# A graph network's edge stage: a table built from its source in place, two result buffers, eight smaller gather parts, another order of work

## The chip, the cores and the metric

The kernel runs on one NeuronCore of a Trainium2 chip. The metric is the device time of one execution in microseconds (us), the median of several runs. TensorE is called PE here, VectorE DVE, ScalarE ACT, GpSimd POOL and SyncE SP.

## The reference, cut to what matters

The program is two graph layers on 50000 nodes with 16 features and 850000 edges sorted by target, each with a residual and a layer norm. The first layer works on groups of eight nodes and has a weight for each of five edge types; the second is two relational convolutions with eight edge types.

```
Wg  = W[edge_types - 1]                              # layer 0
msg = einsum('eoi,eib->eob', Wg, xr[src])
y   = segment_sum(msg, dst) + segment_sum(Bv[edge_types - 1], dst)
x   = layernorm(x + y)
for r in range(8):                                   # layer 1, done twice
    msg = msg + where(edge_type == r, x[src] @ W[r], 0)
agg = segment_sum(msg * norm, dst);  h = agg + x @ root + bias
x   = layernorm(x + log_softmax(h))
```

## The kernel before, in words

Instead of multiplying each edge's source row by its type's weight, the kernel first writes a table in DRAM: for each node (or group of eight) one row per edge type, already multiplied. A layer then gathers one table row per edge and sums by target. The program is a chain of stages with a barrier between them: stage_edges, stage_sum0, stage_x1, stage_layer (l1), stage_middle, stage_layer (l2), stage_output.

stage_edges does four things side by side, each engine by a list of instructions written out by hand and held together by semaphores.

1. The table of layer 0. `x_sb` holds the source, 49 tiles of 128 groups (WINS0 = 49). For each tile ACT copies the tile into a staging buffer `xt` (L266), PE transposes it (L308), ACT copies the transposed tile back (L274), PE multiplies it with `mix` and adds the bias row by a matmul with one row (L317, L318; 512 + 128 columns), ACT copies the result from PSUM to `out` (L278, L279), and SP stores `out` (L214). `xt`, `x_turned`, `turn_ps` and `out` have two buffers each, `mul_ps` has one.
2. The steps. The 7040 steps by which the layers walk over the edges are found from the last target of each tile of 128 edges: DVE counts (L368, L371), PE sums the counts over the partitions with one matmul (L300, `bend_ps`), DVE compares and counts again (L387 to L402, `steps_ready`), then fills the small step tables (to L425, `tables_ready`).
3. The local targets of each step. POOL gathers the target rows of the steps (L108 by way of `fetch`, 64 indirect DMAs in PARTS = 4 parts of 16) into one buffer `got`, DVE subtracts the window's first node (L441), PE transposes in 16 batches of four (L340), ACT casts them into `env.local` (L291). Part b may be gathered when part b-1 has been transposed (`got_turned`).
4. The lists of table rows, one for layer 0 and one for layer 1. DVE computes `flat` (L429 to L435, L450), PE transposes it in 13 batches (L329), ACT casts them into `typ6` or `typ8` (L285), SP stores them (L227, L229).

PE's order is: L300, the whole table, the whole list of layer 0, the 16 batches of local targets, the list of layer 1. ACT's order is the same. On SP the loads of x, of the targets and of the edge lists stand ahead of the 49 stores of the table, and the small step tables and the lists' stores stand behind them.

The class Table builds the tables of layers 1 and 2 (in stage_x1 and stage_middle) in the same manner, with staging copies (L649), a transpose (L627), a copy back (L655) and matmuls of 512 + 512 + 128 columns (L638), but with two result buffers, and with DVE reading a part of each result (L675, L677).

## Time and profile before

| what | value |
|---|---|
| median of 3 runs | 19951.57 us (19948.39 to 19953.89) |
| the profiled execution | 19956.64 us |
| its span | 19954.9 us |
| PE, DVE, ACT, POOL busy | 44%, 20%, 1%, 69% of the span |
| stage_edges | from 0 to 531.57 us of the span |

The span is the time from the first to the last instruction of the profiled execution; the rest of its time lies around it. All start times below are us from the span's start. PEld is PE's weight load, which overlaps its matmuls; a matmul in f32 is issued as two passes, and a transpose as one. Engines whose name ends in q are the engine's queue, which issues waits and DMAs.

### The profile page before, as it was taken

What the parts mean: (1) busy time and instruction counts of PE and PEld (TensorE: products, weight loads), DVE (VectorE), ACT (ScalarE), POOL (GpSimd) and SP (SyncE); (2) the same over time, 40 slices, a digit from 0 to 9 for tenths busy, and PEclk for the clock granted to TensorE, in tenths of its full rate; (3) what the DMA queues carried; (4) which work ended last, traced back from release to release, by engine and by line L of the source; (5) the groups of instructions that cost most, each with busy time, mean ns of one, the idle gap of its engine ahead of it and who ended that gap; (6) DMA issues with size and microseconds to landing.
All of it is one profiled execution on the core that took longest, in us unless ns stands there. A gap on an engine that the chain in (4) does not pass through costs nothing. (4 is left out here: it accounts for less than half of the span.)

```text
span 19954.9 us, 176031 instructions
## 1 busy us (share of the span) xinstructions
PE 8832.7 (44%) x35275; PEld 7745.8 (39%) x35276; DVE 3970.6 (20%) x4654; ACT 265.0 (1%) x590; POOL 13732.8 (69%) x14217
## 2 busy tenths in 40 slices
PE   6565054444444444444445444444444444444444
PEld 2343054344334433444344333443344434443444
DVE  2223921111111111111112211111111111111113
ACT  1000000000000000000000000000000000000000
POOL 1672877777777777777770577777777777777760
PEclk9556555555555555555555655555555555555555
DMA  2122100000000000000000300000000000000000
GB/s 80 53 53 97 9 8 7 7 7 7 7 7 7 7 7 7 7 7 7 7 7 1 64 7 7 7 7 7 7 7 7 7 7 7 7 7 7 7 6 7
DMA packets 659119, 295.78 MB, mean 15 GB/s; under 512 B 351447, under 2 KB 628204, under 8 KB 657794
## 3 DMA queue, kind: packets, MB, share of 16 engines
q0 software_dynamic: 455680, 168.10, 7.7%
q1 hardware_dynamic: 202690, 124.50, 2.5%
q14 instruction: 317, 2.60, 0.0%
q8 instruction: 30, 0.49, 0.0%
q10 hardware_dynamic: 402, 0.09, 0.0%
HBM read 207.97 MB, written 87.17 MB: 15 GB/s over the span
## 5 line engine op out<-in xcount | busy, mean ns | idle before, releaser
L108 POOL DMA_INDIRECT l_rows<-table,l_idx x13312 | 12862.2, 966 | 4952.9 <-issue 4054.7
L988 PE MATMUL l_ps<-l_rows,l_hot 128*128 x28160 | 6326.9, 375 | 0.0
L988 PEld LDWEIGHTS l_ps<-l_rows,l_hot 128*128 128x128 f32 x28160 | 6137.4, 330 | 395.0 <-issue 395.0
L985 PE MATMUL l_ps<-l_zero 1*128 1x128 f32 x3520 | 1339.9, 482 | 9697.2 <-issue 9627.7
L985 PEld LDWEIGHTS l_ps<-l_zero 1*128 1x128 f32 x3520 | 872.8, 306 | 9835.7 <-issue 9758.4
L1019 DVE TENSOR_TENSOR all_big<-all_big,l_ps 128x128 f32 x1760 | 506.8, 288 | 10839.5 <-PE l_ps L988 10839.5
L1025 DVE TENSOR_TENSOR l_hot<-l_ps,all_local 128x1024 f32<-128x1024 f32 x1760 | 2123.7, 1217 | 5.8 <-issue 5.6
L108 POOL DMA_INDIRECT s_rows<-table,s_idx x832 | 785.6, 944 | 320.7 <-issue 251.3
L1038 DVE TENSOR_TENSOR l_rows<-l_rows,l_ps 128x1024 f32<-128x1024 f32 x208 | 254.0, 1221 | 3542.8 <-DMA l_rows<-table,l_idx 3542.2
L514 PE MATMUL s_ps<-s_zero 1*128 1x512 f32 x448 | 343.8, 906 | 440.1 <-issue 378.2
L517 PEld LDWEIGHTS s_ps<-s_rows,s_hot 128*128 128x128 f32 x1792 | 373.4, 317 | 140.8 <-issue 140.8
L517 PE MATMUL s_ps<-s_rows,s_hot 128*128 x1792 | 403.6, 416 | 0.0
L108 POOL DMA_INDIRECT ed_got<-dst_d,ed_step_i x64 | 83.8, 1310 | 406.7 <-PE ed_turn_ps L340 282.1
L514 PEld LDWEIGHTS s_ps<-s_zero 1*128 1x128 f32 x448 | 107.1, 264 | 558.6 <-issue 543.1
L539 DVE TENSOR_TENSOR early_acc<-early_acc,s_ps 128x1024 f32 x112 | 136.8, 1221 | 875.7 <-PE s_ps L517 875.7
L815 PE MATMUL l_ps<-all_ident,all_big 128*128 128x128 f32 x52 | 14.0, 433 | 349.3 <-DVEq L904 347.6
L815 PEld LDWEIGHTS l_ps<-all_ident,all_big 128*128 128x128 f32 x52 | 9.4, 218 | 353.6 <-DVEq L904 347.7
L318 PE MATMUL ed_mul_ps<-ed_bias_row,ed_one_row 1*128 1x512 f32 x196 | 140.3, 817 | 0.0
L317 PE MATMUL ed_mul_ps<-ed_mix,ed_x_turned 128*128 128x512 f32 x196 | 135.9, 797 | 1.2 <-ACT ed_x_turned L274 1.0
L545 DVE TENSOR_TENSOR s_hot<-s_iota_ps,all_local 128x1024 f32<-128x1024 f32 x112 | 134.0, 1217 | 3.9 <-issue 3.9
L649 ACT COPY midt_xt<-all_big 128x128 f32<-128x128 f32 x49 | 15.1, 310 | 8530.4 <-DVEq L1080 8530.4
L1109 ACT ACT_TABLE_LOAD x7 | 9.0, 1283 | 8752.9 <-PEq L90 8752.8
(172 smaller groups left out, 1815.0 us busy)
## 6 DMA issues: line engine op xcount, KB each, us to landing
l_rows<-table,l_idx POOLq DMA_INDIRECT x13312, 2.3
table<-midt_out SPq DMA_DIRECT2D x49, 512.0 KB
table<-x1t_out SPq DMA_DIRECT2D x48, 512.0 KB, 2.7
table<-ed_out SPq DMA_DIRECT2D x48, 320.0 KB, 2.1
s_rows<-table,s_idx POOLq DMA_INDIRECT x832, 2.6
idx_d<-ed_typ SPq DMA_DIRECT2D x2, 3328.0 KB, 9.4
l_idx<-idx_d SPq DMA_DIRECT2D x208, 32.0 KB, 1.8
ed_typ<-in_edge_type_dram SPq DMA_DIRECT2D x2, 2912.0 KB
```

The costliest lines, as they stand in the source:

```text
L108: pool.indirect_dma_start(out=out[:, j, :], out_offset=None, in_=table, in_offset=bass.IndirectOffsetOnAxis(ap=idx[:, j:j + 1], axis=0)).t ...
L317: nc.tensor.matmul(mul_ps[:, k, 0:z - a], x_turned[:, t % 2, :], mix[:, a:z], start=True, stop=False)
L318: last = nc.tensor.matmul(mul_ps[:, k, 0:z - a], one_row[:, :], bias_row[:, a:z], start=False, stop=True)
L514: nc.tensor.matmul(ps[g % 2][:, c * 512:(c + 1) * 512], zero[:, 0:P], zero[:, :], start=True, stop=False, skip_group_check=True)
L517: last = nc.tensor.matmul(ps[g % 2][:, bass.ds((v % GROUP) * ROW0, ROW0)], hot[:, g % 2, j, :], rows[:, bass.ds(v // GROUP, 1), :].rearran ...
L539: nc.vector.tensor_tensor(at, at, ps[g % 2][:, :].rearrange("n (w f) -> n w f", f=ROW0), ALU.add).then_inc(added, 1)
L545: nc.vector.tensor_tensor(hot[:, g % 2, :, :], iota_ps[:, 0:P].unsqueeze(1).to_broadcast([P, GROUP, P]), local.unsqueeze(2).to_broadcast([ ...
L985: nc.tensor.matmul(sums[g % 2], zero[:, :], zero[:, :], start=True, stop=False, skip_group_check=True)
L988: last = nc.tensor.matmul(sums[g % 2][:, bass.ds((v % GROUP) * FEAT, FEAT)], hot[:, g % 2, j, :], rows[:, bass.ds(v // GROUP, 1), :].rearr ...
L1019: nc.vector.tensor_tensor(at, at, sums[g % 2].rearrange("n (w f) -> n w f", f=FEAT), ALU.add).then_inc(added, 1)
L1025: nc.vector.tensor_tensor(hot[:, g % 2, :, :], lane_ps.unsqueeze(1).to_broadcast([P, GROUP, P]), local.unsqueeze(2).to_broadcast([P, GROUP ...
L1038: nc.vector.tensor_tensor(at, at, scale_ps.unsqueeze(2).to_broadcast([P, SPAN, FEAT]), ALU.mult).then_inc(scaled, 1)
```

## The change

In stage_edges:
- PE transposes the table's source straight from `x_sb`; the staging copies, their buffer and their semaphore go. The class Table loses them too, in both tables that it builds.
- `mul_ps` gets a second buffer; PE may multiply tile t when tile t-2 has been read. `bend_ps` no longer has a bank of its own and uses that of a list buffer. ACT turns back tile t before it reads the result of tile t-1.
- DVE makes `mix` and `bias_row` before it counts, no longer after; PE starts the table when these and x are there.
- L300 moves from the front of PE's list to behind tile 15 (EARLY = 16), and the two-tile loop is begun anew behind it.
- `got` gets a second buffer; PARTS goes from 4 to 8, so a part is 8 gathers and has half the size. Part b waits for part b-2 to be transposed.
- Behind the table PE and ACT do parts 0 and 1 of the local targets, six batches of list 0, part 2, the other seven batches, parts 3 to 7, list 1.

```diff
-PARTS = 4
+PARTS = 8
+EARLY = 16
...
-        got = s.sb("got", [P, SPAN // PARTS, P], I32)
+        got = s.sb("got", [P, 2, SPAN // PARTS, P], I32)
...
-        mul_ps = s.ps("mul_ps", [P, 2, 512])
-        bend_ps = s.ps("bend_ps", [P, 512])
+        mul_ps = [s.ps(f"mul_ps{b}", [P, 2, 512]) for b in range(2)]
         wide_ps = [s.ps(f"wide_ps{b}", [P, 4, P]) for b in range(2)]
+        bend_ps = wide_ps[0][:, :, :].rearrange("p a b -> p (a b)")
...
             for b in range(PARTS):
-                if b:
-                    pool.wait_ge(got_turned, b * part // 4)
-                fetch(pool, got[0:SPANS], rows, step_i[0:SPANS, b * part:(b + 1) * part], part, got_in[b])
+                if b > 1:
+                    pool.wait_ge(got_turned, (b - 1) * part // 4)
+                fetch(pool, got[0:SPANS, b % 2], rows, step_i[0:SPANS, b * part:(b + 1) * part], part, got_in[b])
...
         @block.scalar
...
+            def table_rows(a, z):
+                for t in range(a, z):
+                    act.wait_ge(turned, t + 1)
+                    if t > 1:
+                        act.wait_ge(multiplied, t - 1)
+                    nc.scalar.copy(x_turned[:, t % 2, :], turn_ps[t % 2][:, 0:P]).then_inc(back, 1)
+                    if t > a:
+                        read(t - 1)
+                read(z - 1)
...
+            table_rows(0, EARLY)
+            table_rows(EARLY, WINS0)
             act.wait_ge(idx0_ready, 1)
...
+            local_slots(0)
+            local_slots(1)
+            turned_lists(typ6, 0, 0, 6)
+            local_slots(2)
+            turned_lists(typ6, 0, 6, batches)
+            for b in range(3, PARTS):
+                local_slots(b)
             act.wait_ge(idx1_ready, 1)
-            turned_lists(typ8, batches)
+            turned_lists(typ8, batches, 0, batches)
...
         @block.tensor
...
+            pe.wait_ge(x_in, 32)
 
             def turn(t):
-                pe.wait_ge(staged, t + 1)
                 if t > 1:
                     pe.wait_ge(back, t - 1)
-                nc.tensor.transpose(turn_ps[t % 2][:, 0:P], xt[:, t % 2, :], env.ident[:, :]).then_inc(turned, 1)
...
+                nc.tensor.transpose(turn_ps[t % 2][:, 0:P], x_sb[:, t, :], env.ident[:, :]).then_inc(turned, 1)
+
+            def table_rows(a, z):
+                turn(a)
+                for t in range(a, z):
+                    if t + 1 < z:
+                        turn(t + 1)
+                    pe.wait_ge(back, t + 1)
+                    if t > 1:
+                        pe.wait_ge(read_out, t - 1)
+                    for k, (c, d) in enumerate(((0, 512), (512, width))):
+                        nc.tensor.matmul(mul_ps[t % 2][:, k, 0:d - c], x_turned[:, t % 2, :], mix[:, c:d],
+                                         start=True, stop=False)
+                        last = nc.tensor.matmul(mul_ps[t % 2][:, k, 0:d - c], one_row[:, :], bias_row[:, c:d],
+                                                start=False, stop=True)
+                    last.then_inc(multiplied, 1)
...
+            table_rows(0, EARLY)
+            pe.wait_ge(below_ready, 1)
+            nc.tensor.matmul(bend_ps[:, 0:WINS], ones[:, :], below[:, :], start=True, stop=True
+                             ).then_inc(bend_ready, 1)
+            table_rows(EARLY, WINS0)
             pe.wait_ge(back, WINS0)
...
+            local_slots(0)
+            local_slots(1)
+            pe.wait_ge(steps_ready, 1)
+            turn_lists(idx0_ready, 0, 0, 6)
+            local_slots(2)
+            turn_lists(idx0_ready, 0, 6, batches)
+            for b in range(3, PARTS):
+                local_slots(b)
+            turn_lists(idx1_ready, batches, 0, batches)
```

## Rows read from the trace of the kernel before

**Rows 1.** Busy time by stretch: us, PE, PEld, DVE, ACT, POOL, PEclk, DMA share, GB/s.

```profile
78.70:389.00 310.30, 262.49 (x417) 100.41 (x418) 55.35 (x26) 52.00 (x185) 35.38 (x16) 1.00 0.14 52
389.00:531.57 142.57, 37.94 (x166) 26.11 (x164) 13.97 (x5) 61.15 (x42) 48.43 (x48) 0.56 0.20 70
```

**Rows 2.** Timeline, one tile of layer 0's table: start us, us, what [idle before].

```profile
66.91 0.59 ACT L278 COPY ed_out<-ed_mul_ps 128x512 f32<-128x512 f32 x1 [5.62 <-PE ed_mul_ps L318]
...
67.55 0.31 ACT L266 COPY ed_xt<-ed_x_sb 128x128 f32<-128x128 f32 x1
...
67.91 0.48 PE L308 MATMUL ed_turn_ps<-all_ident,ed_xt 128*128 128x128 f32 x1 [1.04 <-ACT ed_xt L266]
```

**Rows 3.** Timeline: first staging copy, first store, third tile's read.

```profile
22.11 0.50 ACT L266 COPY ed_xt<-ed_x_sb 128x128 f32<-128x128 f32 x2 [15.38 <-DMA ed_x_sb<-in_x_dram]
...
60.95 0.36 SPq L214 DMA_DIRECT2D table<-ed_out  x1
...
78.71 0.59 ACT L278 COPY ed_out<-ed_mul_ps 128x512 f32<-128x512 f32 x1 [10.68 <-DMA table<-ed_out]
```

**Rows 4.** Busy time by stretch, columns as in rows 1.

```profile
76.00:80.00 4.00, 0.28 (x2) 0.29 (x2) 4.00 (x1) 1.12 (x4) 0.00 (x0) 1.00 0.09 32
```

**Rows 5.** Timeline, last tile to last gather of stage_edges.

```profile
388.24 0.59 ACT L278 COPY ed_out<-ed_mul_ps 128x512 f32<-128x512 f32 x1 [5.61 <-PE ed_mul_ps L318]
...
389.34 14.60 ACT L285 CAST ed_typ<-ed_wide_ps 128x512 int32<-128x512 f32 x13 [0.35 <-PE ed_wide_ps L329]
...
409.22 1.01 POOL L108 DMA_INDIRECT ed_got<-dst_d,ed_step_i  x1 [261.24 <-PE ed_turn_ps L340]
...
440.39 1.01 POOL L108 DMA_INDIRECT ed_got<-dst_d,ed_step_i  x1 [10.45 <-PE ed_turn_ps L340]
...
491.22 1.01 POOL L108 DMA_INDIRECT ed_got<-dst_d,ed_step_i  x1 [0.30 <-issue]
```

**Rows 6.** Timeline, last subtraction and first VectorE instruction of the next stage.

```profile
493.77 2.29 DVE L441 TENSOR_TENSOR ed_got<-ed_got,ed_step_w 110x2048 f32<-110x2048 int32 x1 [28.83 <-DMA ed_got<-dst_d,ed_step_i]
...
531.57 0.48 DVE L526 MEMSET s_zero<- 1x512 f32 x1 [27.77 <-PEq L90]
```

**Rows 7.** Timeline: the counting matmul, the first gather, the first subtraction.

```profile
52.12 1.64 PE L300 MATMUL ed_bend_ps<-ed_below,ed_ones 128*128 128x391 f32 x2 [52.12 <-DVEq L373]
...
108.02 1.18 POOL L108 DMA_INDIRECT ed_got<-dst_d,ed_step_i  x1 [106.26 <-DVEq L402]
...
149.85 2.29 DVE L441 TENSOR_TENSOR ed_got<-ed_got,ed_step_w 110x2048 f32<-110x2048 int32 x1 [17.20 <-DMA ed_got<-dst_d,ed_step_i]
```

**Rows 8.** Timeline of PE: list transposes, and matmuls of layer 1's table.

```profile
388.14 1.97 PE L329 MATMUL ed_wide_ps<-all_ident,ed_flat 128*128 128x128 f32 x8
...
395.48 0.66 PE L329 MATMUL ed_wide_ps<-all_ident,ed_flat 128*128 128x128 f32 x4 [0.25 <-ACT ed_typ L285]
...
503.91 1.97 PE L329 MATMUL ed_wide_ps<-all_ident,ed_flat 128*128 128x128 f32 x8 [1.48 <-DVEq L452]
...
1796.44 4.21 PE L638 MATMUL x1t_mul_ps<-x1t_mix,x1t_x_turned 128*128 128x512 f32 x6
...
1803.09 2.10 PE L638 MATMUL x1t_mul_ps<-x1t_mix,x1t_x_turned 128*128 128x512 f32 x6
```

**Rows 9.** Busy time by stretch, columns as in rows 1.

```profile
504.00:508.00 4.00, 3.41 (x14) 2.66 (x15) 0.00 (x0) 3.86 (x4) 0.00 (x0) 0.50 0.00 0
```

**Rows 10.** Timeline of VectorE and GpSimd, one gather beside a tensor_tensor.

```profile
125.56 7.09 DVE L435 TENSOR_TENSOR ed_flat<-ed_flat,ed_typ 128x6656 f32<-128x6656 f32 x1
...
125.95 7.58 POOL L108 DMA_INDIRECT ed_got<-dst_d,ed_step_i  x1 [0.31 <-issue]
```

**Rows 11.** Waits, the middle table: who waited for whom, us, times, longest.

```profile
ACT midt_out L667 <- DMA table<-midt_out: 61.0, 46, 3.1
...
PEld midt_turn_ps L627 <- ACT midt_xt L649: 8.3, 18, 1.9
```

**Rows 12.** The page's DMA issues: transfers, KB each, median us to landing.

```profile
table<-ed_out SPq DMA_DIRECT2D x48, 320.0 KB, 2.1
```

More of the change, by code:

```diff
@@ L260, in _, with read @@
             act.dma_start(env.ident[:, :], env.eye).then_inc(small_in, 16)
-            act.wait_ge(x_in, 32)
-            def stage(t):
-                if t > 1:
-                    act.wait_ge(turned, t - 1)
-                nc.scalar.copy(xt[:, t % 2, :], x_sb[:, t, :]).then_inc(staged, 1)
-            stage(0)
-            for t in range(WINS0):
-                if t + 1 < WINS0:
-                    stage(t + 1)
-                act.wait_ge(turned, t + 1)
-                if t > 1:
-                    act.wait_ge(multiplied, t - 1)
-                nc.scalar.copy(x_turned[:, t % 2, :], turn_ps[t % 2][:, 0:P]).then_inc(back, 1)
+            def table_rows(a, z):
[7 more added lines that the diff above has]
+                read(z - 1)
+            def read(t):
                 act.wait_ge(multiplied, t + 1)
@@ L363, in _ @@
             st.wait()
-            cmp = flat[:, :].bitcast(BF16)
-            for a, z in ((0, 256), (256, WINS)):
-                n = z - a
-                view = cmp[:, 0:n * PER].rearrange("p (w k) -> p w k", k=PER)
-                st(nc.vector.tensor_tensor(view, last_w[:, :].unsqueeze(1).to_broadcast([P, n, PER]),
-                                           win_id[:, a:z].unsqueeze(2).to_broadcast([P, n, PER]), ALU.is_le))
-                st.wait()
-                st(nc.vector.tensor_reduce(below[:, a:z], view, AX.X, ALU.add))
-                st.wait()
-            dve.sem_inc(below_ready, 1)
             dve.wait_ge(small_in, 16 * (CH + 2))
@@ L384, in _ @@
             dve.sem_inc(mix_ready, 1)
+            cmp = flat[:, :].bitcast(BF16)
+            for a, z in ((0, 256), (256, WINS)):
+                n = z - a
+                view = cmp[:, 0:n * PER].rearrange("p (w k) -> p w k", k=PER)
+                st(nc.vector.tensor_tensor(view, last_w[:, :].unsqueeze(1).to_broadcast([P, n, PER]),
+                                           win_id[:, a:z].unsqueeze(2).to_broadcast([P, n, PER]), ALU.is_le))
+                st.wait()
+                st(nc.vector.tensor_reduce(below[:, a:z], view, AX.X, ALU.add))
+                st.wait()
+            dve.sem_inc(below_ready, 1)
             dve.wait_ge(bend_ready, 1)
@@ L643, in act @@
         nc = self.nc
-        act.wait_ge(self.values_ready, 1)
-        def stage(t):
-            if t > 1:
-                act.wait_ge(self.turned, t - 1)
-            nc.scalar.copy(self.xt[:, t % 2, :], self.values[:, t, :]).then_inc(self.staged, 1)
         def turn_back(t):
@@ L655, in turn_back @@
             nc.scalar.copy(self.x_turned[:, t % 2, :], self.turn_ps[t % 2][:, 0:P]).then_inc(self.back, 1)
-        stage(0)
-        stage(1)
         turn_back(0)
@@ L661, in act @@
                 turn_back(t + 1)
-            if t + 2 < WINS0:
-                stage(t + 2)
             act.wait_ge(self.multiplied, t + 1)
```

77 lines of the change are left out of this document (29 added, 48 removed).

## The prediction, made before the changed kernel had run

> **What bounds the kernel.** I read the page first: the two layer stages run at the pace of GpSimd's gathers, and this change touches neither, so its worth has to be read in stage_edges, which ends where the next stage's first VectorE instruction starts, 531.57 us into the span [rows 6], and in the two tables built by class Table. Then the busy times by stretch, to see who is dense where. From 78.7 to 389 us PE is busy 262.49 of 310.30 us: the table of layer 0 [rows 1]. From 389 to 531.57 it is busy 37.94 of 142.57, and the stretch is a relay of GpSimd, VectorE, PE and ScalarE [rows 1].
>
> In the first stretch the timeline of one tile shows the loop. ScalarE reads the single result buffer after 5.62 us of waiting for PE, then stages the source, turns back, and PE idles 1.04 us until the staging copy [rows 2]. The last 46 reads span 388.24 - 78.71 us, so a tile takes 6.73 us, and PE works for 6.73 - 1.04 = 5.69 of it [rows 2, 3, 5]. The first two tiles are special: the third tile's read waits 10.68 us for the store of the first, until 78.71 [rows 3], and the DMA share has fallen to 0.09 just then [rows 4]: the edge lists' loads stand ahead of the table's stores.
>
> In the second stretch the turning of list 0 (14.60 us on ScalarE) comes first, and the second part of the step gathers starts only at 409.22, after four turned batches [rows 5]. A gather takes 1.01 + 0.30 = 1.31 us. Between two parts of 16 GpSimd waits 10.45 us, since one buffer holds a part until it is turned [rows 5]. The last gather starts at 491.22; 2.55 us later VectorE subtracts, the list of layer 1 is made, turned and stored, and the stage ends at 531.57 [rows 5, 6].
>
> **The change, part by part.**
>
> *Earlier start.* The mix is built ahead of the counting and PE waits for x alone, so tile 0 can start at about 22.1, where the first staging copy starts now [rows 3]. Two tiles fit into the two `out` buffers, two more into the result buffers, then ScalarE waits for the first store. That one is queued on the same SP ring behind the same loads, so it lands about when it does now; I take 78.71 (bounds 76 to 80, the stretch in which the DMA engines run empty) [rows 3, 4]. The start 32 us earlier is worth two tiles, not 32 us.
>
> *Two result buffers, no staging.* The loop of a tile then holds only PE's own 5.69 us: the idle 1.04 goes with the staging copy and the read [rows 2]. Turning back tile t and reading tile t-1 (about 1.1 us of ScalarE a tile) lie under the 5.6 us of the other buffer's matmuls. After 78.71: read and turn-back 1.1, then tile 4 and 44 more at 5.69: 78.71 + 1.1 + 45 x 5.69 = 335.9. The moved matmul L300 (1.64 us [rows 7]) and the restart of the two-tile pipeline behind it, some 1.0, add 2.6: PE ends the table at 338.4. It ends now with the read at 388.24, so 49.8 us are won. Bounds: 5.64 (a tile packed tighter) to 5.8 us, 333 to 345.
>
> *Later steps.* L300 goes from 52.12 to behind tile 15, at 79.8 + 12 x 5.69 = 148. VectorE queues behind it everything from the steps on, and GpSimd waits for that: gathers now start at 108.02 and the first subtraction is at 149.85 [rows 7]. All this moves 96 us later, the first 16 gathers to 204 to 246. It costs nothing while the table covers it: PE wants them at 338. Cover left: about 90 us; without it each microsecond costs one. The mix's wait for the small loads now stands ahead of the counting on VectorE; a delay there has the same cover.
>
> *Order behind the table.* Parts 0 and 1 (16 gathers) are ready, so PE turns two batches at once, and GpSimd may start part 2: 2.0 us (eight passes [rows 8]) plus 0.3 after 338.4, at 340.7. Now that start is 21.0 us behind the last read (409.22 - 388.24), because list 0 and four batches come first. List 0 is put between the parts: 13 batches at 14.60/13 = 1.12 us plus 16 local batches at 2.0 are 47 us of ScalarE in some 70 us of gathers, hidden. The tightest place is part 5's start, behind the last seven list batches (7.9 us) and part 3; I find 3 to 4 us of slack there, and take 0 (bounds 0 and 5). SP's store of list 0 now falls beside gathers; they issue on another queue and have 5 us before they are wanted: 0.
>
> *Two gather buffers.* Six parts of eight, 48 gathers without the two gaps of 10.45: 47 x 1.31 = 61.6 us to the last start. Against it stands what GpSimd loses to VectorE: the gather at 125.95 took 7.58 us in place of 1.01, until 0.9 us after a tensor_tensor that read two SBUF operands [rows 10]. The subtraction L441 is such an operation. Now GpSimd stands idle while it runs; with two buffers five of them (parts 2 to 6, half of 2.29 = 1.15 us each) run while GpSimd gathers: 5 x 1.15 = 5.75 us. I take it in full, since the row shows a whole stall; bounds 0 and 7. In the Trainium skill, SBUF — State Buffer, Who interferes with whom, a tensor_tensor with two SBUF inputs is said to contend with a GpSimd instruction that reads SBUF, while a probe is reported in which tensor_tensor did not stall a DMA issued there. By the probe the term would be 0 and the sum 5.75 lower; the trace here disagrees with the probe, 7.58 us against 1.01.
>
> *Tail.* From L441 to the stage's end 531.57 - 493.77 = 37.8, now with half the subtraction: 36.65 [rows 6]. Sum: 340.7 + 61.6 + 5.75 + 2.55 + 36.65 = 447.3 against 531.57: 84.3 us won.
>
> *The other tables.* In the middle table ScalarE waits for a store 46 times of 49, 61.0 us in all; the loads of PE that wait for a staging copy, 18 with 8.3 us, follow those waits [rows 11]. Removing the copy does not make a store land earlier: the first tile's staging, about 0.5 us in each table, is sure. I take 1 us for both (bounds: 4 lost by a clock that falls in another place, 8 won).
>
> Total 85.3. The profiled execution took 19956.6 us (span 19954.9), 5 above the median of the runs, 19951.6; the difference is set against the median: **19866 us**.
>
> **The rivals.**
>
> *The clock rises* (0.06). PE would now be without a gap for 250 us. The trace prints 1.00 throughout the table, but eight passes of a transpose take 1.97 at 388.14 and the same 1.97 at 503.91, where the clock's row says 0.50, and from 395.48 four take 0.66 [rows 8, 9]. So I read the table as run at the lower level, 1.2 GHz, and the 1.00 as a state that was not recorded before the first change. At 2.4 GHz a tile would take half (in the next table six passes go from 4.21 to 2.10 us [rows 8]): the last 44 tiles 125 us less, the stage's end at about 322, 19741 us. For it: the idle 1.04 us disappears. Against it: PE was 85% busy for 310 us [rows 1] and the clock didn't rise; it rose only some 7 us after the work had changed to transposes that use all rows, while two of the four matmuls of a tile, here and after, use a single row (L318). The Trainium skill, TensorE: Matmul & The Clock Gate, Part 1, says that sustained activity releases the throttle and asks for no gaps; by it the table would run at the higher level and give this 19741.
>
> *The result buffer isn't the limit* (0.05): the tile stays at 6.73, since ScalarE's order binds. The table ends at 391, only the second stretch is won, 32 us: 19919. Against it: the class Table has two result buffers and its passes follow without a gap there, 2.10 us a tile [rows 8].
>
> *The parts stall on each other* (0.04): each part waits until the one before is turned behind list batches, 7 us for six parts: 42 lost, 19908.
>
> *Slower, stores that pile up* (0.03): the stores of the table leave from 29 us on and land as late as the first does now, 17.7 us after the copy (60.95 to 78.7 [rows 3]), for the whole table. With two `out` buffers a tile would take 8.9 us, the table would end at 488, and the stage at 597: 65 slower, 20017. It decides from about 7.5 us a tile, landings over 15 us. Against it: a store of 320 KB lands in 2.1 us by the median, and the DMA share behind 78.7 is 0.14 [rows 1, 12].
>
> **How the numbers follow.** My forecast has 0.80; 0.02 is left for what I don't see. Its own range: 6 less without the lock, 5 less and 7 more from the tile's pace and the store, 5 from the hand-over of parts, -7 to +5 from the other tables: 19848 to 19884. The range given, 19836 to 19897, adds some room for a cost that no row shows; the rivals at 19741, 19908, 19919 and 20017 (0.18) lie outside. A change below 0.2% (40 us) counts as none. Faster: 0.80 + 0.06, part of the two rivals near the bound and half of the unseen, 0.89; same 0.07; slower 0.04.
>
> **What the changed profile would show.** First matmul of the table near 22 us, a PE gap from about 46 to 80, then a read every 5.7 us; L300 near 148; GpSimd's first gather near 204; the table's end near 338; the seventeenth gather at 341, gathers up to 7 stretched by about 1.2 us each by L441; the next stage's first VectorE instruction near 447; the other two tables within 4 us of before. A tile of 2.9 us, a first store that lands far from 79, or waits of GpSimd between parts would each make a term wrong.

## The result and the profile after

| what | before | after |
|---|---|---|
| median (5 runs each, side by side) | 19952.75 us (19948.39 to 19954.55) | 19850.43 us (19844.47 to 19854.65) |
| ratio, 95% interval | | 0.9949 [0.9934, 0.9963] |
| the profiled execution, its span | 19956.64, 19954.9 us | 19848.08, 19846.3 us |
| stage_edges ends | 531.57 us | 434.45 us |

The change wins 102.3 us by the medians, 0.5%. The forecast was 19866, 15.6 above the measurement, which lies in the range (19836 to 19897) and in the forecast's own (19848 to 19884). By the two profiles stage_edges is 97.1 us shorter, and the rest of the span 11.5. Line numbers below are those of the changed kernel: L313 is the transpose, L324 and L326 the matmuls, L267 turns back, L276 and L277 read the result, L352 counts, L109 gathers, L462 subtracts.

Busy time by stretch after the change, in the columns of [rows 1]:

```profile
22.00:46.00 24.00, 23.22 (x38) 8.70 (x38) 23.93 (x3) 2.32 (x8) 0.00 (x0) 1.00 0.97 259
46.00:77.50 31.50, 0.00 (x0) 0.00 (x0) 7.91 (x2) 0.01 (x1) 0.00 (x0) 1.00 0.89 216
77.50:331.00 253.50, 252.39 (x408) 95.72 (x409) 80.38 (x29) 42.77 (x138) 35.39 (x16) 1.00 0.17 63
331.00:434.45 103.45, 40.51 (x167) 29.80 (x165) 14.52 (x7) 62.35 (x44) 49.73 (x48) 1.00 0.30 96
```

PE works from 22 to 46 us, is idle for 31.5 us, and is then busy 252.39 of 253.50 us: the table runs without a gap. The DMA share is 0.97 and 0.89 in the first two stretches, 0.70 from 70 to 74 us and 0.11 from 76 to 77.5: the engines run empty just before the third read.

The timeline of ScalarE at the third tile's read, which answers to [rows 3]; of PE there and one tile later; of ScalarE at the last read, which answers to [rows 5]:

```profile
77.49 0.58 ACT L276 COPY ed_out<-ed_mul_ps 128x512 f32<-128x512 f32 x1 [42.70 <-DMA table<-ed_out]
```
```profile
78.47 2.07 PE L324 MATMUL ed_mul_ps<-ed_mix,ed_x_turned 128*128 128x512 f32 x2 [33.11 <-ACT ed_x_turned L267]
80.47 2.07 PE L326 MATMUL ed_mul_ps<-ed_bias_row,ed_one_row 1*128 1x512 f32 x2
82.47 0.80 PE L324 MATMUL ed_mul_ps<-ed_mix,ed_x_turned 128*128 128x128 f32 x2
83.20 0.79 PE L326 MATMUL ed_mul_ps<-ed_bias_row,ed_one_row 1*128 1x128 f32 x2
83.92 0.47 PE L313 MATMUL ed_turn_ps<-all_ident,ed_x_sb 128*128 128x128 f32 x1
84.19 1.92 PE L324 MATMUL ed_mul_ps<-ed_mix,ed_x_turned 128*128 128x512 f32 x2
...
89.48 0.47 PE L313 MATMUL ed_turn_ps<-all_ident,ed_x_sb 128*128 128x128 f32 x1
```
```profile
330.59 0.58 ACT L276 COPY ed_out<-ed_mul_ps 128x512 f32<-128x512 f32 x1 [4.70 <-PE ed_mul_ps L326]
```

From transpose to transpose a tile takes 89.48 - 83.92 = 5.56 us, against 6.73 before. The start comes 32 us earlier and then waits 42.70 us for the first store.

The second half: the first gather behind the table, the only two that take longer than 1.15 us from there on, and the last; VectorE's subtractions beside them; the stage's end, which answers to [rows 6]:

```profile
332.51 1.01 POOL L109 DMA_INDIRECT ed_got<-dst_d,ed_step_i  x1 [91.67 <-PE ed_turn_ps L347]
...
346.98 1.36 POOL L109 DMA_INDIRECT ed_got<-dst_d,ed_step_i  x1 [0.30 <-issue]
...
355.22 1.01 POOL L109 DMA_INDIRECT ed_got<-dst_d,ed_step_i  x1 [0.30 <-issue]
...
372.30 1.94 POOL L109 DMA_INDIRECT ed_got<-dst_d,ed_step_i  x1 [0.30 <-issue]
...
395.57 1.01 POOL L109 DMA_INDIRECT ed_got<-dst_d,ed_step_i  x1 [0.30 <-issue]
```
```profile
346.24 1.23 DVE L462 TENSOR_TENSOR ed_got<-ed_got,ed_step_w 110x1024 f32<-110x1024 int32 x1 [102.58 <-DMA ed_got<-dst_d,ed_step_i]
355.20 1.28 DVE L462 TENSOR_TENSOR ed_got<-ed_got,ed_step_w 110x1024 f32<-110x1024 int32 x1 [7.74 <-DMA ed_got<-dst_d,ed_step_i]
372.13 1.23 DVE L462 TENSOR_TENSOR ed_got<-ed_got,ed_step_w 110x1024 f32<-110x1024 int32 x1 [15.65 <-DMA ed_got<-dst_d,ed_step_i]
...
398.20 1.22 DVE L462 TENSOR_TENSOR ed_got<-ed_got,ed_step_w 110x1024 f32<-110x1024 int32 x1 [9.26 <-DMA ed_got<-dst_d,ed_step_i]
...
434.45 0.48 DVE L547 MEMSET s_zero<- 1x512 f32 x1 [27.71 <-PEq L91]
```

48 gathers follow without a wait between parts (0.30 us of issue each), 63.1 us from the first start to the last.

### The profile page after: what moved, and what is told of

It is laid out like the page before. It is cut to its first block and busy times, and to the rows that moved or that the text cites. A ratio compares the mean times of both kernels' runs of the same rounds, so it can differ in the third digit from the quotient of the medians.

```text
span 19846.3 us, 175756 instructions
## 1 busy us (share of the span) xinstructions
PE 8826.6 (44%) x35275; PEld 7745.4 (39%) x35276; DVE 3972.9 (20%) x4658; ACT 236.6 (1%) x443; POOL 13724.6 (69%) x14217
## 5 line engine op out<-in xcount | busy, mean ns | idle before, releaser
L109 POOL DMA_INDIRECT l_rows<-table,l_idx x13312 | 12853.3, 966 | 4950.9 <-issue 4056.6
L109 POOL DMA_INDIRECT s_rows<-table,s_idx x832 | 785.1, 944 | 319.3 <-issue 251.1
L109 POOL DMA_INDIRECT ed_got<-dst_d,ed_step_i x64 | 85.1, 1330 | 309.7 <-DVEq L423 199.1
L324 PE MATMUL ed_mul_ps<-ed_mix,ed_x_turned 128*128 128x512 f32 x196 | 133.6, 785 | 33.4 <-ACT ed_x_turned L267 33.1
L326 PE MATMUL ed_mul_ps<-ed_bias_row,ed_one_row 1*128 1x512 f32 x196 | 140.3, 817 | 0.0
L869 DVE TENSOR_SCALAR_CACHE_REDUCE all_big<-all_big 128x6656 bf16<-128x6656 bf16 x16 | 113.4, 7086 | 0.6
```

What stands on the lines that cost most here:

```text
L109: pool.indirect_dma_start(out=out[:, j, :], out_offset=None, in_=table, in_offset=bass.IndirectOffsetOnAxis(ap=idx[:, j:j + 1], axis=0)).t ...
L324: nc.tensor.matmul(mul_ps[t % 2][:, k, 0:d - c], x_turned[:, t % 2, :], mix[:, c:d], start=True, stop=False)
L326: last = nc.tensor.matmul(mul_ps[t % 2][:, k, 0:d - c], one_row[:, :], bias_row[:, c:d], start=False, stop=True)
```

## The experiments

All times of stages are from one profiled execution each, us of the span; "stage end" is the first instruction of the next stage, as 434.45 above. Edits are to the changed kernel where nothing else is said; line numbers in their rows can stand a few off those above, and some diffs show only a part of the edit, marked by "...". One thing scatters from profile to profile whatever the edit, the landing of the table's first store, and so the third read: in the nine profiles with the early start and the loads in their old place (the changed kernel's and those of eight runs below) it lies between 72.51 and 79.47 us, and the table's end moves with it. Differences of up to 7 us between last reads or stage ends are therefore read from the third read on, or behind the last read.

### The table's half alone

```diff
-PARTS = 8
+PARTS = 4
...
-        got = s.sb("got", [P, 2, SPAN // PARTS, P], I32)
+        got = s.sb("got", [P, 1, SPAN // PARTS, P], I32)
...
-            local_slots(0)
-            local_slots(1)
-            turn_lists(idx0_ready, 0, 0, 6)
-            local_slots(2)
-            turn_lists(idx0_ready, 0, 6, batches)
-            for b in range(3, PARTS):
+            turn_lists(idx0_ready, 0, 0, batches)
+            for b in range(PARTS):
                 local_slots(b)
```

> The changed kernel with the gather side put back: four parts of 16 gathers, one gather buffer, list 0 ahead of all local targets. Only the table half of the change is left (source in place, two result buffers, early mix, the counting matmul behind tile 15). Theory, the two halves add up: the table ends at about 331 us as in the changed kernel, and the relay behind it takes what it took before, 531.57 - 388.24 = 143.3 us, so the stage ends at 474, 57 us earlier than before, and the kernel is at about 19888 us. Rival, the halves need each other (the later steps cost something when the parts are large): the stage ends later than 480.

19892.17 us, ratio 0.997 [0.9959, 0.9981]. Last read 325.61, stage end 468.04: 63.5 us of the 97.1. Some 5 us of that are the first store's, since the third read is at 72.51 in this profile and at 77.49 in the changed kernel's. Behind the last read the stage takes 142.4 us here, 143.3 before and 103.9 in the changed kernel. So the table's half carries some 58 us and the gathers' half 39; by the medians the second is 41.7.

### One result buffer

```diff
-        mul_ps = [s.ps(f"mul_ps{b}", [P, 2, 512]) for b in range(2)]
+        mul_ps = [s.ps("mul_ps0", [P, 2, 512])] * 2
...
-                    if t > 1:
-                        pe.wait_ge(read_out, t - 1)
+                    if t:
+                        pe.wait_ge(read_out, t)
```

> The changed kernel with one result buffer in stage_edges; PE may multiply a tile when the tile before has been read. Theory, the second result buffer gives the tile's pace: PE waits for the two reading copies (0.65 us and the hand-over), a tile takes about 6.2 to 6.3 us in place of 5.56, the table ends some 32 us later, the stage at about 466, the kernel at about 19882. Rival, the pace came from leaving out the staging copies: a tile stays below 5.8 us and the stage ends at 435 to 445.

19899.17 us, 0.9972 [0.9961, 0.9983]; last read 374.50, stage end 478.06. PE's timeline of one tile:

```profile
90.36 0.47 PE L313 MATMUL ed_turn_ps<-all_ident,ed_x_sb 128*128 128x128 f32 x1
91.36 2.04 PE L324 MATMUL ed_mul_ps<-ed_mix,ed_x_turned 128*128 128x512 f32 x2 [0.53 <-ACT ed_out L277]
...
96.78 0.47 PE L313 MATMUL ed_turn_ps<-all_ident,ed_x_sb 128*128 128x128 f32 x1
```

With the staging copy gone but one buffer, PE waits for the read of the result, and a tile takes 6.42 us. That is more than the 6.2 to 6.3 expected, and the stage ends 12 us later than expected. Of the 1.17 us by which the tile became shorter, staging and ScalarE's new order are 0.31 and the second buffer, put in behind them, 0.86; the second buffer with the staging kept was not run.

### The staged tables of the class Table

The class Table is that of the kernel before; stage_edges is as changed.

> The changed kernel with the class Table as it was before (staging copies in the tables of layers 1 and 2), stage_edges unchanged. In the two profiles the stage of layer 1's table went from 194.1 to 191.2 us and the middle table's span from 126.9 to 123.0 us. Theory, that is the staging: with it back the two are 194 and 127 within 1 us. Rival, it is where the clock and the stores happened to fall: they come out at 191 and 123, or scattered by several us. In both cases stage_edges ends at 434 to 435 and the kernel is within 10 us of the changed one.

19852.71 us, 0.995 [0.9933, 0.9967], 2.3 us over the changed kernel, whose own runs spread over 10. The two stages that build these tables (the second read up to the issue of its last store) took 191.24 and 122.95 us in the profile of the changed kernel, 193.03 and 127.69 here, 194.19 and 126.80 before. Over the eleven profiles with the unstaged class the first lies between 189.56 and 193.68 (mean 191.7) and the second between 122.73 and 127.04 (124.8); over the three with the staged one, this, the kernel before and its variant below, the means are 193.5 and 127.0. That is some 2 us a table, less than what single profiles scatter (4 us in each of the two).

### The late start

The mix is built behind the counting again, and the counting matmul stands at the front of PE's list.

```diff
+            pe.wait_ge(below_ready, 1)
+            nc.tensor.matmul(bend_ps[:, 0:WINS], ones[:, :], below[:, :], start=True, stop=True
+                             ).then_inc(bend_ready, 1)
...
-            table_rows(0, EARLY)
-            pe.wait_ge(below_ready, 1)
-            nc.tensor.matmul(bend_ps[:, 0:WINS], ones[:, :], below[:, :], start=True, stop=True
-                             ).then_inc(bend_ready, 1)
-            table_rows(EARLY, WINS0)
+            table_rows(0, WINS0)
```

> The changed kernel with the old front: the counting, then the counting matmul, then the mix, then the table in one piece, so PE starts the table at about 54 us, not 22. Theory, the start is worth next to nothing, since ScalarE waits for the first store until 77.5 in the changed kernel and 78.7 before: the third tile is read at about 78.7, the restart behind tile 15 (2.1 us) falls away, and the stage ends at 433 to 436. Rival, the 32 us of earlier start count: the stage ends at 445 to 465.

19851.98 us, 0.9948 [0.9932, 0.9965]; last read 327.02, stage end 431.78, 2.7 us earlier than the changed kernel's. PE's first matmul of the table is at 54.31 in place of 22.76, and the steps' first gather at 107.7 again. The third read is at 75.96, and the fourth follows at 76.76 as in the changed kernel (78.29 behind 77.49): four tiles are ready when the first store lands, in either case. From the third read to the last it takes 251.1 us in place of 253.1, since the two-tile loop is not begun anew. The early start and the move of the counting matmul are worth nothing here.

### The steps later still

`EARLY = 40`, one execution.

> The changed kernel with EARLY = 40: the counting matmul stands behind tile 39, at about 279 us in place of 145, so all steps come 134 us later, the first gather at about 335. Theory, the later steps are covered for some 87 us (in the changed kernel the second part's subtraction ends at 243.7 and PE wants it at 331) and cost one for one beyond: 134 - 87 = 47 us if every gather waits, somewhat less (about 41) since later parts follow without a gap. The stage ends at 475 to 482. Rival, there is no such cover (the changed kernel already lost some of it): the stage ends near 434 + 134 = 568. Rival, the steps are not on the path at all: 435 to 440.

The counting matmul runs at 276.17, the first gather at 332.07, stage end 474.14: 39.7 us later. The steps moved 131.2 us and cost 39.7. From the first gather to the last (435.31) GpSimd never waits in this run, so each further microsecond would cost one, and the cover in the changed kernel was 131.2 - 39.7 = 91.5 us, against "about 90" in the prediction. Outside stage_edges this execution shows both layer stages some 17 us longer, which the edit does not touch.

### A second operation that reads two SBUF operands

```diff
+                if 2 <= b < PARTS - 1:
+                    st(nc.vector.tensor_tensor(x_sb[:, 0:32, :], x_sb[:, 0:32, :], x_sb[:, 0:32, :], ALU.max))
```

> The changed kernel, and behind the subtraction of parts 2 to 6 VectorE does one more operation that the result doesn't need: a tensor_tensor of 4096 elements with two SBUF operands (about 4.3 us each, on the table's source, which is no longer wanted). Theory A, a gather that begins while such an operation runs is held until its end, whatever the length: each of the five adds 3 to 4.3 us to the gathers, 15 to 21 us in all, gathers of 4 to 5 us are seen, the last gather starts at 410 to 416 in place of 395.6, the stage ends at 450 to 456. Theory B, a tensor_tensor does not hold gathers and the two longer gathers of the changed kernel (1.36 and 1.94 us) have another cause: the last gather starts at 395 to 397 and the stage ends at 434 to 436.

One execution: last gather 411.96, 16.4 us later, stage end 450.20. VectorE and GpSimd side by side:

```profile
346.28 1.28 DVE L462 TENSOR_TENSOR ed_got<-ed_got,ed_step_w 110x1024 f32<-110x1024 int32 x1 [100.94 <-DMA ed_got<-dst_d,ed_step_i]
347.70 4.42 DVE L469 TENSOR_TENSOR ed_x_sb<-ed_x_sb 128x4096 f32<-128x4096 f32 x1
```
```profile
347.62 1.01 POOL L109 DMA_INDIRECT ed_got<-dst_d,ed_step_i  x1 [0.31 <-issue]
348.93 4.08 POOL L109 DMA_INDIRECT ed_got<-dst_d,ed_step_i  x1 [0.30 <-issue]
353.32 1.01 POOL L109 DMA_INDIRECT ed_got<-dst_d,ed_step_i  x1 [0.30 <-issue]
```

The gather that begins 0.08 us ahead of the long operation takes 1.01 us; the next begins inside it and ends at 353.01, 0.89 us behind the operation's end at 352.12. So a gather that begins inside is held until the operation is over, and what it loses is what is left of it. From restart to last gather it takes 78.8 us in place of 63.1.

### The same with a reduction

```diff
+                if 2 <= b < PARTS - 1:
+                    st(nc.vector.tensor_reduce(last_w[:, 0:32], x_sb[:, 0:32, :], AX.X, ALU.max))
```

> As the run with the additional tensor_tensor, but the additional operation is a tensor_reduce over the same 4096 elements, of the same length, with one SBUF operand. Theory A, only the second SBUF operand (or a fast mode) holds the gathers: the last gather starts at 395 to 397 and the stage ends at 434 to 436. Rival, any long VectorE operation holds them: 410 to 416 and 450 to 456.

One execution: last gather 395.35, stage end 434.19, as without the operation. It too takes 4.42 us (345.88 to 350.30), and the gathers beside it take 1.01. From restart to last gather it takes 64.5 us, 1.4 more than in the changed kernel, and all of that stands beside the subtractions: four gathers of 1.30 to 2.03 us. It is the kind of operation that holds a gather, not its length. What of the kind does it these two runs don't separate: the reduction has one SBUF operand in place of two, and writes 32 elements in place of 4096. A second SBUF operand is not needed, as the changed kernel's own trace shows at an earlier place:

```profile
203.68 4.03 POOL L109 DMA_INDIRECT ed_got<-dst_d,ed_step_i  x1 [0.30 <-issue]
```
```profile
203.96 3.63 DVE L450 TENSOR_SCALAR ed_flat<-ed_typ 128x6656 f32<-128x6656 int32 x1 [0.22 <-DVE ed_step_w L444]
```

This tensor_scalar reads one SBUF operand. The gather begins 0.28 us ahead of it, ends at 207.71, 0.12 us behind it, and takes 4.03 us. The kernel's total, 19889.02, is not read here: both layer stages are some 16 us longer in this execution as well.

### The edge lists' loads on another queue

```diff
-            sp.wait_ge(padded, 5)
-            load_list(sp, src, env.src, src_in)
-            load_list(sp, typ6, env.type6, type6_in)
-            load_list(sp, typ8, env.type8, type8_in)
...
+            act.wait_ge(x_in, 32)
+            act.wait_ge(padded, 5)
+            load_list(act, src, env.src, src_in)
+            load_list(act, typ6, env.type6, type6_in)
+            load_list(act, typ8, env.type8, type8_in)
```

> The changed kernel with the loads of the three edge lists issued by ScalarE (behind its wait for x) and no longer by SP, so that the table's stores no longer stand behind them in SP's queue. Theory, the first store waited for its place in the queue: now it lands well before 77.5, at 40 to 55 us, PE's idle stretch of 33 us shrinks to 0 to 15, the table ends 20 to 30 us earlier (about 303 to 311), and the stage ends at 405 to 415. Rival, it waited for the DMA engines' bandwidth, which are busy until about 75 whoever issues: the first store still lands near 77, and the stage ends at 432 to 440.

19848.25 us, 0.9945 [0.9928, 0.9962]. The stores of the table no longer stand behind these loads on SyncE's queue, and still the third read comes only at 71.22, 6.3 us earlier than in the changed kernel's profile and 1.3 below the lowest of the nine; the fourth waits again:

```profile
71.22 0.59 ACT L277 COPY ed_out<-ed_mul_ps 128x512 f32<-128x512 f32 x1 [32.86 <-DMA table<-ed_out]
...
75.68 0.59 ACT L277 COPY ed_out<-ed_mul_ps 128x512 f32<-128x512 f32 x1 [3.53 <-DMA table<-ed_out]
```

The DMA share is 1.03 from 22 to 46 us and 0.96 from 46 to 71.2. The first store waits for the engines' bandwidth far more than for its place in a queue. The stage ends at 423.51, 10.9 us earlier in the profiles; by the medians the kernel is 2.2 us faster, which is inside the spread. Of the 12.1 us by which the last read (318.5) is earlier, 6.3 are the store's; the rest is a short rise of the clock, which the edit did not ask for. PE's timeline behind tile 15, where the counting matmul (L353) and a new start of the loop put passes that use all rows side by side, and the busy times with the granted clock:

```profile
138.70 1.67 PE L353 MATMUL ed_wide_ps<-ed_below,ed_ones 128*128 128x391 f32 x2
...
144.60 0.34 PE L314 MATMUL ed_turn_ps<-all_ident,ed_x_sb 128*128 128x128 f32 x1
...
147.61 0.33 PE L314 MATMUL ed_turn_ps<-all_ident,ed_x_sb 128*128 128x128 f32 x1
...
151.70 0.47 PE L314 MATMUL ed_turn_ps<-all_ident,ed_x_sb 128*128 128x128 f32 x1
```
```profile
146.00:148.00 2.00, 2.00 (x8) 0.97 (x8) 2.00 (x1) 0.28 (x1) 0.00 (x0) 1.00 0.42 164
200.00:320.00 120.00, 120.00 (x201) 46.46 (x200) 21.58 (x6) 20.49 (x65) 30.61 (x14) 0.50 0.18 64
```

The tile from 144.60 to 147.61 takes 3.01 us; the clock falls at about 149 while PE goes on without a gap, and from then on it stands recorded at 0.50 with tiles of 5.56 us, the same as in the changed kernel, whose column prints 1.00. The run with the reduction shows the same rise at the same place (one tile of 4.24 us); the other profiles of this front don't.

### The bias matmul over all rows

`one_row` becomes 128 rows with a one in the first and zeros below, `bias_row` the same with the bias: the same sum, made by a matmul that uses all rows of the array.

```diff
-        bias_row = s.sb("bias_row", [1, width])
-        one_row = s.sb("one_row", [1, P])
+        bias_row = s.sb("bias_row", [P, width])
+        one_row = s.sb("one_row", [P, P])
...
-            nc.vector.memset(one_row[:, :], 1.0)
+            st(nc.vector.memset(one_row[:, :], 0.0))
+            st(nc.vector.memset(bias_row[:, :], 0.0))
...
+            st(nc.vector.memset(one_row[0:1, :], 1.0))
...
```

> The changed kernel, and the bias is added by a matmul over all 128 rows (ones in the first row of the weights and zeros below, the bias in the first row of the operand and zeros below), with the same columns and passes as the one-row matmul before; the result is the same. Theory, PE's clock stayed at 1.2 GHz in the table because half of its passes used a single row: now all passes use all rows, the clock rises within the first dense tiles after 78 us, a tile takes about 2.8 us in place of 5.56, the table ends near 207, and since the counting matmul also comes earlier (about 115) the stage ends at 315 to 325 and the kernel is at about 19735. Rival, the kind of rows doesn't matter, and a clock for this stretch is not to be had: tiles stay at 5.4 to 5.7 us and the stage ends at 430 to 437.

19727.73 us (19723.45 to 19731.43), 0.9887 [0.9871, 0.9904]: 122.7 us faster than the changed kernel. Last read 187.01, stage end 308.93. Busy time by stretch, the granted clock in the seventh column, and ScalarE's reads:

```profile
79.00:100.00 21.00, 19.55 (x65) 11.03 (x66) 0.00 (x0) 7.70 (x25) 0.00 (x0) 0.82 0.33 127
100.00:187.00 87.00, 86.73 (x342) 49.86 (x340) 74.53 (x27) 34.62 (x113) 20.08 (x5) 1.00 0.38 145
```
```profile
85.12 0.58 ACT L276 COPY ed_out<-ed_mul_ps 128x512 f32<-128x512 f32 x1 [3.90 <-PE ed_mul_ps L326]
...
88.23 0.58 ACT L276 COPY ed_out<-ed_mul_ps 128x512 f32<-128x512 f32 x1 [2.19 <-PE ed_mul_ps L326]
...
90.50 0.58 ACT L276 COPY ed_out<-ed_mul_ps 128x512 f32<-128x512 f32 x1 [1.35 <-PE ed_mul_ps L326]
```

A tile takes 2.27 us (88.23 to 90.50) in place of 5.56, with the same number of columns; 2.8 was expected. The clock was at its lower level while PE waited for the store, and rose during the second tile after it had resumed (3.11 us between the reads at 85.12 and 88.23). The table ends 143.6 us earlier and the stage 125.5: the steps are late now, GpSimd's 64 gathers run from 165.70 to 270.42 without a wait, and the rest of the cover is gone. PE's first tile after the wait, still at the recorded lower level:

```profile
80.44 2.08 PE L324 MATMUL ed_mul_ps<-ed_mix,ed_x_turned 128*128 128x512 f32 x2 [47.35 <-ACT ed_x_turned L267]
82.31 1.92 PE L326 MATMUL ed_mul_ps<-ed_bias_row,ed_one_row 128*128 128x512 f32 x2
84.02 0.63 PE L324 MATMUL ed_mul_ps<-ed_mix,ed_x_turned 128*128 128x128 f32 x2
...
85.09 1.80 PE L324 MATMUL ed_mul_ps<-ed_mix,ed_x_turned 128*128 128x512 f32 x2
```

From first matmul to first matmul it takes 85.09 - 80.44 = 4.65 us; the tile behind the wait in the changed kernel, with its one-row matmuls, takes 84.19 - 78.47 = 5.72. So the full bias shortens the tile twice: by some 1.1 us at the lower clock (0.75 at the higher one, 3.02 us between two reads in the run with the lists on another queue and 2.27 here), and by the clock.

### The same in the kernel before

> The kernel before, with the same bias matmul over all 128 rows and nothing else changed. PE keeps its gap of about 1 us behind every tile (one result buffer, staging). Theory, the rows decide and not the gap: the clock rises here too, a tile takes about 2.8 + 1.0 = 3.8 us in place of 6.73, and the table ends at 245 to 260 in place of 388. Rival, the gap matters too: the clock stays at the lower level and the tile at 6.5 to 6.8 us, or the clock goes up and down and the mean tile is between 4.5 and 6.

One execution, 19809.82 us: the bias over all rows in the kernel before, with its staging copies and its one result buffer. Last read 246.69, stage end 389.58, a tile 3.64 us in place of 6.73. PE's timeline and busy time:

```profile
149.76 0.33 PE L308 MATMUL ed_turn_ps<-all_ident,ed_xt 128*128 128x128 f32 x1 [1.04 <-ACT ed_xt L266]
...
153.40 0.33 PE L308 MATMUL ed_turn_ps<-all_ident,ed_xt 128*128 128x128 f32 x1 [1.04 <-ACT ed_xt L266]
```
```profile
100.00:247.00 147.00, 105.43 (x371) 58.02 (x370) 34.45 (x24) 44.75 (x160) 35.38 (x16) 1.00 0.26 97
```

The gap of 1.04 us is there in every tile and PE is busy only 72% of the time, and the clock is at 1.00, in a trace whose column has recorded changes ahead of this stretch (0.50 from 70 to 79 us). It is the one-row matmuls that kept it low, not the gap.

### All of it together

The bias over all rows, `EARLY = 4`, the loads of the source list and of layer 0's list on ScalarE behind x, the load of layer 1's list on SyncE behind the 49 stores.

> The changed kernel with the bias matmul over all rows, as in the run before, and two more edits: the source of the edge lists and the list of layer 0 are loaded by ScalarE behind x, the list of layer 1 by SyncE behind the 49 stores of the table; and the counting matmul stands behind tile 3 in place of tile 15. Theory (the first store waits for what the loads take of the DMA engines, so fewer bytes ahead of it bring it forward): first store read at 60 us (bounds 55 to 71), the table at 2.27 us a tile ends at 167 to 178, the counting matmul near 65 to 70, the first 16 gathers are done at 150, the last gather 63 us behind the table's end, the stage ends at 273 to 285 against 308.9, and the kernel takes 19695 to 19705. Rival one: the transfers still share the engines, and the first store lands at 71 to 76: stage end 285 to 300, kernel 19705 to 19720. Rival two: with a short table the late list of layer 1 is missing where the list of layer 1 is turned, and the stage ends no earlier than 305.

19695.22 us (19690.89 to 19700.27), 0.9871 [0.9855, 0.9888] against before: 255.7 us faster, and 32.5 below the run with the full bias. The third read is at 61.39, the last at 167.80, stage end 278.38. The first store comes 11 to 18 us ahead of the nine profiles, and 9.8 ahead of the run in which the loads were only moved to the other queue: that is what the bytes taken out ahead of it are worth. But the load that was put off comes back:

```profile
168.88 0.81 SPq L125 DMA_DIRECT2D ed_typ<-in_edge_type_dram  x2
```
```profile
193.47 1.23 DVE L467 TENSOR_TENSOR ed_got<-ed_got,ed_step_w 110x1024 f32<-110x1024 int32 x1 [40.46 <-DMA ed_got<-dst_d,ed_step_i]
```
```profile
196.84 1.01 POOL L109 DMA_INDIRECT ed_got<-dst_d,ed_step_i  x1 [7.32 <-PE ed_turn_ps L349]
```

It is issued as the gathers restart (168.82). The subtraction of part 2, whose last gather was issued at 178.0, waits for its rows until 193.47, and GpSimd then waits 7.32 and 1.19 us between parts. The DMA share is 1.07 from 172 to 178 us and 0.98 from 178 to 184. From restart to last gather it takes 70.0 us in place of 63.1; that this load is what held the rows was not tested by itself.

### One gather buffer, eight parts, the new order

```diff
-        got = s.sb("got", [P, 2, SPAN // PARTS, P], I32)
+        got = s.sb("got", [P, 1, SPAN // PARTS, P], I32)
...
-                if b > 1:
-                    pool.wait_ge(got_turned, (b - 1) * part // 4)
+                if b:
+                    pool.wait_ge(got_turned, b * part // 4)
```

> The changed kernel with one gather buffer of eight gathers in place of two; eight parts and the new order of PE and ScalarE stay. Theory (the two buffers are what removes GpSimd's waits between parts, order and size alone do not): every part waits until the one before is turned, about 15.4 us a part in place of 10.5, more where list batches stand between; last gather at 434 to 445, stage end 473 to 484 against 434.5, that is no better than the table's edits alone (468.0). Rival: the new order and the smaller parts carry the gain, the second buffer little: last gather at 396 to 402, stage end 434 to 441.

One execution, 19887.01 us: last gather 431.12, stage end 468.52, which is that of the table's half alone (468.04). Each further part waits:

```profile
346.23 1.01 POOL L109 DMA_INDIRECT ed_got<-dst_d,ed_step_i  x1 [6.15 <-PE ed_turn_ps L347]
...
361.35 1.01 POOL L109 DMA_INDIRECT ed_got<-dst_d,ed_step_i  x1 [4.92 <-PE ed_turn_ps L347]
```

and 56 gathers instead of 48 stand behind the table. Behind the last read (327.95) the stage takes 140.6 us, against 142.4 for the table's half alone and 103.9 for the changed kernel: the smaller parts and the new order bring next to nothing by themselves, and the second buffer on top of them brings 34 to 37 us. What the second buffer would bring without them, with parts of 16 in the old order, was not run. The last gather is 3 us below the range expected: a part takes 361.35 - 346.23 = 15.1 us against 15.4, and only one part waits longer because of list batches.

## Why the prediction was right, and where its terms were off

**Two result buffers, no staging.** The mechanism was as forecast, the size a little better: last read 330.59, 57.6 us earlier, against 49.8. I took a tile as 6.73 - 1.04 = 5.69, PE's own work; it is 5.56, below my bound of 5.64. When PE no longer stops after each tile, the last pass pair (0.79 us) overlaps the next transpose by 0.07, and the first matmul takes 1.92 in place of 1.98. Over 44 tiles that is 5.7 us; the store that lands 1.2 earlier is most of the rest. The rival that the buffer is not the limit is refuted by the run with one buffer: without the second one, 43.6 of the 97.1 us are gone. Nor do the parts stall on each other: there is no wait of GpSimd behind 332.51.

**Earlier start.** "Worth two tiles, not 32 us" was still too much. The kernel with the late start loses nothing by it: it too has four tiles ready when the first store lands, and its stage ends 2.7 us earlier. What has the fourth tile ready is the second result buffer; in the kernel before, with one, the fourth read comes 6.73 us behind the third. The reason that I gave was also not the main one: I put the first store behind the loads because it is on the same queue. With the loads on another queue it lands only 6.3 us earlier, which is hardly outside the scatter of the nine profiles; with 3.3 MB less ahead of it, 9.8 more. The number (78.71 forecast, 77.49 measured) was good because the trace showed when the DMA engines ran empty [rows 4], and that it came within 1.2 us is luck, since this landing scatters over 7.

**Later steps.** L352 at 144.97 (148 forecast), the first gather at 200.88 (204), no cost; the cover measured by the run with EARLY = 40 is 91.5 us (90). Beyond it a microsecond costs one.

**Order and buffers.** GpSimd restarts at 332.51, 1.9 us behind the last read, as forecast (2.3), and does not wait between parts. The run with one gather buffer shows that without the second one neither the smaller parts nor the order does this; that the second one would do it alone is not shown. The tail from the last subtraction to the end is 434.45 - 398.20 = 36.25 (36.65).

**What GpSimd loses to VectorE.** 5.75 us forecast, 63.1 - 61.7 = 1.4 measured. The row I leaned on [rows 10] showed a true thing, a gather held until 0.9 us behind the operation, and I made of it a whole operation's length for each subtraction. Beside a subtraction only a gather that begins inside it is held, and only for the rest; GpSimd's own gathers are 1.31 us apart and the subtraction is 1.23 long, so a subtraction costs between nothing (355.20, where a gather begins 0.02 us behind its start and is not held) and 0.93 us (372.13), in the run with the reduction up to 1.02. The runs with a second operation show both sides: a tensor_tensor of 4.42 us stretches a gather to 4.08, a reduction of 4.42 us none. The tensor_scalar rows show that a gather can be held by an operation that it began ahead of, and by one with a single SBUF operand; the prediction had neither. The Trainium skill, SBUF — State Buffer, Who interferes with whom, says that tensor_reduce does not contend on trn2 and that a tensor_tensor with two SBUF inputs contends with GpSimd's reads: these runs agree with both. The probe that it reports, in which tensor_tensor did not stall a DMA, does not carry over to these gathers, which take 4.08 us against 1.01; the page does not say whether its DMA was an indirect one, as these are.

**The other tables.** 1 us forecast; by the two profiles the sum of the two stages fell by 6.8, which is within the bound of 8. The runs put the gain at about 2 us a table, at the edge of what can be told.

**Where the rest is.** By the profiles 108.6 us were won, 23.3 more than the sum: 12.8 in stage_edges (table 7.8, GpSimd's wait 4.3, hand-over and tail 0.7), 5.8 in the other tables and 4.7 in stages that the change does not touch. Both are of the size of the scatter. The medians give 102.3, 17.0 more than the sum.

**The rival of the clock** did not come about, for the reason given. PE was busy 252.39 of 253.50 us, and the tile of 5.56 us is that of the lower level, 1.2 GHz, as the run with the lists on another queue shows, where the column reads 0.50 beside it. The Trainium skill, TensorE: Matmul & The Clock Gate, Part 1, promises the higher level for such activity; with one-row matmuls the trace disagrees, with all rows it agrees (2.27 us a tile). The prediction had priced it at 19741 from the next table's rows; with the full bias it measured 19727.7. That these two lie close is luck: half a tile's time was priced (2.8 us), the tile became shorter still (2.27), and 18 us of the table's gain were lost again because the steps came too late.

**Slower, stores that pile up**: nothing of it even at 2.27 us a tile, where the pace stays PE's.

## What to carry to other kernels

Before an engine's idle gaps are closed, ask which clock its busy time runs at, and read that from durations of the same pass elsewhere in the trace. Here closing the gaps was worth 57.6 us and filling the rows of a bias matmul 122.7 more, for two operands filled up with zeros. When a stage starts earlier, look at what its first output waits for: if the DMA engines are full then, the earlier start buys nothing, and only fewer bytes ahead of it do. A second buffer removes a wait between producer and consumer; smaller parts and another order without it may change nothing, so test them apart.

## What the runs showed of the hardware

- A matmul of one row is no cheaper than one of 128 beside it (2.07 us for two passes of 512 columns in both), and a stream in which half of the matmuls have one row did not raise the granted clock in 250 us of unbroken work. With all rows it rose in the first tile at the table's start and in the second after the wait, and in the kernel before it stayed at 1.00 beside a gap in every tile. In two profiles it rose for 3 to 7 us where the counting matmul stands, and fell again in the alternating stream with PE busy throughout.
- A tile fell by more than the clock's factor of two, from 5.56 to 2.27 us, since full and one-row weights in turn cost time of their own. At the lower level the two passes of 512 columns hold PE for 2.00 us in such a stream (78.47 to 80.47 above) and for 1.71 where all matmuls use all rows (82.31 to 84.02); at the higher the whole tile takes 3.02 us in the one and 2.27 in the other. Why they cost it is not known from these runs.
- The clock column prints 1.00 until the first change is recorded: for the changed kernel through the whole of stage_edges, though its tiles take the 5.56 us that stand beside a recorded 0.50 in the run with the lists on another queue. Ahead of that record the column can't be trusted.
- In two of the single executions (EARLY = 40, and the reduction) both layer stages took 15 to 18 us longer, with instructions that the edits do not touch. Such a jump needs no edit: of seven executions of the kernel before that were timed beside these runs, one, which has no profile, took 19984.10 us, 30 above their median of 19953.93. What it was stays open; it is a third of what the change brings, and a single execution can't tell it from an effect.
